# Double-width input products on GpSimd, six replica slots, output rows in the gated tile, and five state products a period on GpSimd

## The reference, cut to what matters

```python
def _mamba(x, inproj, conv_w, conv_b, xproj, dt_w, dt_b, Alog, Dp, outproj):
    u, z = jnp.split(x @ inproj, 2, axis=-1)
    uc = silu(causal_conv(u, conv_w) + conv_b)               # 512 channels
    dt, Bm, Cm = jnp.split(uc @ xproj, [16, 32], axis=-1)     # 16 states
    delta = softplus(dt @ dt_w + dt_b)
    A = -jnp.exp(Alog)
    def step(h, (u_t, d_t, B_t, C_t)):                        # along the sequence
        h = exp(d_t[..., None] * A) * h + (d_t * u_t)[..., None] * B_t[:, None, :]
        return h, einsum('bdn,bn->bd', h, C_t)
    y = (ys + uc * Dp) * silu(z)
    return y @ outproj
```

## Time and profile before

| | |
|---|---|
| median of 3 runs | 1573.46 us (1573.46 to 1575.78) |
| the profiled execution | 1577.74 us |
| its span | 1575.5 us |
| busy: PE, DVE, ACT, GpSimd | 1188.5, 1168.5, 766.0, 917.2 us |
| L1057, 256 input products on GpSimd | 597.3 us, 2364 ns each |
| L1105, 192 + 64 recurrences on DVE | 439.0 + 145.8 us |
| L1115, 192 C products on DVE | 234.9 us, 1223 ns each |
| L1063, 64 C products on GpSimd | 151.1 us, 2361 ns each |

### The profile page before, as it was taken

How to read it: one execution, slowest core, us unless ns; L and a number is a source line. 1 busy time by engine, 2 the same in 40 slices (tenths; PEclk the granted TensorE clock), 3 DMA queues, 4 the chain that set the end, 5 groups by cost and what they waited for, 6 DMA issues and landing times. The chain is left out here.

```text
span 1575.5 us, 14568 instructions
## 1 busy us (share of the span) xinstructions
PE 1188.5 (75%) x4900; PEld 663.6 (42%) x4900; DVE 1168.5 (74%) x1029; ACT 766.0 (49%) x1018; POOL 917.2 (58%) x410
## 2 busy tenths in 40 slices
PE   6899982897659887288883763445663999999998
PEld 4788820232113332033221210111232778787887
DVE  4433356999999999999999999995277654544544
ACT  5333364677555675457755554441134543333440
POOL 4420017999999999999999999983355000000000
PEclk9999995898769998698987766666885999999999
DMA  5133016442365232633233343210502230301102
GB/s 188 47 114 107 27 59 280 147 160 69 147 214 187 76 130 105 253 140 114 108 135 125 153 152 133 88 45 14 208 27 64 97 134 1 134 0 54 66 27 79
DMA packets 44415, 173.73 MB, mean 110 GB/s; under 512 B 5681, under 2 KB 10289, under 8 KB 31554
## 3 DMA queue, kind: packets, MB, share of 16 engines
q1 hardware_dynamic: 44354, 172.98, 29.8%
HBM read 138.89 MB, written 34.08 MB: 110 GB/s over the span
## 5 line engine op out<-in xcount | busy, mean ns | idle before, releaser
L1057 POOL TENSOR_TENSOR scan_dbu<-scan_rep,scan_bc 128x1024 f32<-128x1024 f32 x256 | 597.3, 2364 | 43.2 <-DMA scan_rep<-dd_rows 36.6
L996 ACT ACTIVATE scan_hs<-scan_rep,scan_neg_a 128x1024 f32<-128x1024 f32 x256 | 285.4, 1118 | 347.4 <-DVE scan_hc L1115 305.8
L1105 DVE TENSOR_TENSOR_SCAN scan_hs<-scan_hs,scan_dbu 128x1024 f32<-128x1024 f32 x192 | 439.0, 2286 | 11.3 <-ACT scan_hs L996 10.9
L904 PE MATMUL scan_ysum<-scan_hc,scan_sel 128*32 128x512 f32 x1024 | 176.3, 821 | 236.0 <-DVE scan_hc L1115 235.9
L1115 DVE TENSOR_TENSOR scan_hc<-scan_hs,scan_bc 128x1024 f32<-128x1024 f32 x192 | 234.9, 1223 | 6.1
L904 PEld LDWEIGHTS scan_ysum<-scan_hc,scan_sel 128*32 128x32 f32 x1024 | 36.3, 132 | 356.2 <-issue 356.2
L829 PE MATMUL scan_pb<-scan_xin,scan_inwf 128*128 128x512 f32 x384 | 172.8, 604 | 0.0
L1063 POOL TENSOR_TENSOR scan_hc<-scan_hc,scan_bc 128x1024 f32<-128x1024 f32 x64 | 151.1, 2361 | 12.9 <-DVE scan_hc L1105 12.6
L1105 DVE TENSOR_TENSOR_SCAN scan_hc<-scan_hs,scan_dbu 128x1024 f32<-128x1024 f32 x64 | 145.8, 2278 | 11.2 <-POOL scan_dbu L1057 11.2
L829 PEld LDWEIGHTS scan_pb<-scan_xin,scan_inwf 128*128 128x128 f32 x384 | 72.4, 193 | 103.3 <-issue 103.3
L32 PE MATMUL ffn_sl<-ffn_tanh_s,xm_s 128*128 128x512 f32 x384 | 106.0, 411 | 2.3 <-DVE ffn_tanh_s L1814 2.3
(11 more groups left out here) (186 smaller groups left out, 1626.6 us busy)
## 6 DMA issues: line engine op xcount, KB each, us to landing
scan_rep<-dd_rows SPq DMA_DIRECT2D x64, 1024.0 KB, 5.6
scan_bc<-bc_rows SPq DMA_DIRECT2D x32, 512.0 KB, 5.9
dd_rows<-scan_dd SPq DMA_DIRECT2D x16, 1024.0 KB, 3.8
ffn_wt<-in_ew SPq DMA_DIRECT2D x16, 1024.0 KB, 7.8
scan_inwf<-fold SPq DMA_DIRECT2D x12, 512.0 KB, 3.8
cond<-scan_bc SPq DMA_DIRECT2D x16, 256.0 KB, 3.2
scan_xin<-cond SPq DMA_DIRECT2D x4, 1024.0 KB, 7.5
y_all<-scan_yo SPq DMA_DIRECT2D x8, 512.0 KB, 3.1
```

Source lines behind the costliest of these rows:

```text
L904: mm = nc.tensor.matmul(ysum[i * D32:(i + 1) * D32, h, :], sel[:], hc[:, (s0 + i) % HCR, h * CT:(h + 1) * CT], start=False, stop=last, til ...
L996: nc.scalar.activation(hs[:, s % HSR, :], rep[:, e % REPS, 0, :], ACT.Exp, scale=neg_a[:, k % 2, NI * dc + i, r // NI:r // NI + 1]).then_i ...
L1057: nc.gpsimd.tensor_tensor(dbu[:, s % DBR, :], rep[:, e % REPS, 1, :], bc[:, j, 0, :], ALU.mult).then_inc(dbu_done, 1)
L1105: nc.vector.tensor_tensor_scan(states, hs[:, s % HSR, :], dbu[:, s % DBR, :], 0.0, ALU.mult, ALU.add).then_inc(scan_done, 1)
```

## The change

What it does:
- `inputs` is called for every second unit and computes two input products in one operation: 128 x 2 x 1024, the B row broadcast over both. It waits for both replicas and for both `dbu` buffers.
- `REPS` goes from 5 to 6, so that a pair lies in adjacent slots and does not wrap.
- `pool_unit`: five C products a period on GpSimd in place of four, units 0, 2, 8, 10, 13 (late periods: 0, 2, 4, 10, 13).
- `POOL_STEP_AT` (6, 7) becomes (6, 8), the late one (8, 9) becomes (8, 10), so `step_du` comes behind one more pair.
- To make room in SBUF: `yo` goes and `out_rows` writes over the last two slices of `uc`, which the output projection has read by then; so it first waits for both projections of its half. `conv` of those slices waits for the stores. `ident` lies in `hc`'s last slot. `xw` and `dtw` hold one direction and are loaded again for each group in period 2.

```diff
-REPS = 5
+REPS = 6
+POOL_UNITS, LATE_POOL_UNITS = (0, 2, 8, 10, 13), (0, 2, 4, 10, 13)
+def late_step(w):
+    return w == 0 or w % DC == DC - 1
 def pool_unit(s):
     r = s % UPP
-    return r % NI == 0
+    return r in (LATE_POOL_UNITS if late_step(s // UPP) else POOL_UNITS)
-POOL_STEP_AT, LATE_POOL_STEP_AT = (6, 7), (8, 9)
+POOL_STEP_AT, LATE_POOL_STEP_AT = (6, 8), (8, 10)
...
-        self.xw = sb("xw", [P, 2, DC, XROWS])
-        self.dtw = sb("dtw", [DTR + 1, 2, DIN])
+        self.xw = sb("xw", [P, DC, XROWS])
+        self.dtw = sb("dtw", [DTR + 1, DIN])
...
+    def load_row_weights(self, sp, a, k):
+        sp.dma_start(self.xw[:], a["xw"][:, k % 2]).then_inc(self.rows_w_in, 16)
+        sp.dma_start(self.dtw[:], a["dtw"][:, k % 2]).then_inc(self.rows_w_in, 16)
...
-        yo = sb("yo", [P, KC, CT])
+        ident = hc[:, HCR - 1, 0:P]
...
+        def out_place(k, h):
+            return uc[:, k % 2, DC - KC:DC, h * CT:(h + 1) * CT]
...
@@ SP, in period p of group k
+                    if p == DC - 2 and n < GROUPS:
+                        bank, use = USES["t", k, DC - 1, HALVES - 1]
+                        sp.wait_ge(bank_ready[bank], use)
+                        ahead.load_row_weights(sp, a, n)
...
@@ ACT, conv(k, dc, h)
+                if k >= 2 and dc == DC - KC and h == 0:
+                    act.wait_ge(yo_stored, 16 * HALVES * (k - 1))
@@ ACT
             def out_rows(k, cc, h):
-                n = HALVES * k + h
-                wait(act, yo_stored, 16 * n)
+                for other in range(KC):
+                    ready(act, "o", k, other, h)
                 x, free = ready(act, "o", k, cc, h)
-                nc.scalar.activation(yo[:, cc, :], x, ACT.Copy).then_inc(free, 1)
+                nc.scalar.activation(out_place(k, h)[:, cc, :], x, ACT.Copy).then_inc(free, 1)
@@ GpSimd, inputs(s)
                 if r < NI:
-                    pool.wait_ge(rep_in[e % REPS], 16 * (e // REPS + 1))
+                    for x in (e, e + 1):
+                        pool.wait_ge(rep_in[x % REPS], 16 * (x // REPS + 1))
                 if w % DC == 0 and r % NI == 0:
                     pool.wait_ge(bc_in[j], 2 * 16 * (w // DC + 1))
-                wait(pool, scan_done, s - DBR + 1)
-                nc.gpsimd.tensor_tensor(dbu[:, s % DBR, :], rep[:, e % REPS, 1, :], bc[:, j, 0, :], ALU.mult
-                                        ).then_inc(dbu_done, 1)
+                wait(pool, scan_done, s + 1 - DBR + 1)
+                nc.gpsimd.tensor_tensor(dbu[:, s % DBR:s % DBR + 2, :], rep[:, e % REPS:e % REPS + 2, 1, :],
+                                        bc[:, j, 0, :].unsqueeze(1).to_broadcast([P, 2, SEQ]), ALU.mult
+                                        ).then_inc(dbu_done, 2)
@@ GpSimd, the loop over units
-                    inputs(s)
+                    if r % 2 == 0:
+                        inputs(s)
@@ DVE, weigh(s)
+                if s == HCR - 1:
+                    dve.wait_ge(diag_done, 2 * DC)
```

More of the change, by code:

```diff
@@ L590, in __init__ @@
         self.stored = [[ctx.enter_context(nc.semaphore(f"scan_stored{d}_{cc}")) for cc in range(KC)] for d in range(2)]
-        self.vecs, self.inwz_in, self.folded = (ctx.enter_context(nc.semaphore("scan_" + n)) for n in ("vecs", "inwz_in", "folded"))
+        self.vecs, self.inwz_in, self.folded, self.rows_w_in = (
+            ctx.enter_context(nc.semaphore("scan_" + n)) for n in ("vecs", "inwz_in", "folded", "rows_w_in"))
         self.inwf_in = [ctx.enter_context(nc.semaphore(f"scan_inwf_in{i}")) for i in range(IWR)]
@@ L595, in load_vectors @@
     def load_vectors(self, sp, a):
-        for dst, name in ((self.vec, "vecs"), (self.neg_a, "alog"), (self.one_row, "one_row"), (self.xw, "xw"), (self.dtw, "dtw"),
-                          (self.taps, "taps")):
+        for dst, name in ((self.vec, "vecs"), (self.neg_a, "alog"), (self.one_row, "one_row"), (self.taps, "taps")):
             sp.dma_start(dst[:], a[name]).then_inc(self.vecs, 16)
+        self.load_row_weights(sp, a, 0)
+    def load_row_weights(self, sp, a, k):
+        sp.dma_start(self.xw[:], a["xw"][:, k % 2]).then_inc(self.rows_w_in, 16)
+        sp.dma_start(self.dtw[:], a["dtw"][:, k % 2]).then_inc(self.rows_w_in, 16)
     def load_z_weights(self, sp, a, k):
@@ L630, in mamba_phase @@
         outw = sb("outw", [P, DC, DM])
-        ident, sel = sb("ident", [P, P]), sb("sel", [P, D32])
+        sel = sb("sel", [P, D32])
         diag = sb("diag", [P, 2, DC, P])
@@ L646, in mamba_phase @@
         pb = ps("pb", [P, 2, CT])
-        vecs, inwz_in, inwf_in, xin_in = ahead.vecs, ahead.inwz_in, ahead.inwf_in, ahead.xin_in
+        vecs, inwz_in, inwf_in, xin_in, rows_w_in = ahead.vecs, ahead.inwz_in, ahead.inwf_in, ahead.xin_in, ahead.rows_w_in
         consts_in, outw_in, zeroed, neg_done, diag_done = (sem(n) for n in (
@@ L747, in store_out @@
                 freed(sp, *(("o", k, cc, h) for cc in range(KC)))
-                sp.dma_start(y_all[k][:, :, h * CT:(h + 1) * CT], yo[:]).then_inc(yo_stored, 16)
+                sp.dma_start(y_all[k][:, :, h * CT:(h + 1) * CT], out_place(k, h)).then_inc(yo_stored, 16)
             def z_used(k):
@@ L753, in z_used @@
                     sp.wait_ge(bank_ready[bank], use)
-            for dst, name in ((ident, "ident"), (sel, "sel")):
-                sp.dma_start(dst[:], a[name]).then_inc(consts_in, 16)
+            for dst, name in ((ident, "ident"), (sel[:], "sel")):
+                sp.dma_start(dst, a[name]).then_inc(consts_in, 16)
             store_rows(0)
@@ L847, in first_x_proj @@
                     for h in range(HALVES):
-                        mm = nc.tensor.matmul(out[h][0][0:XROWS, :], xw[:, 0, dc, :], uc[:, 0, dc, h * CT:(h + 1) * CT],
+                        mm = nc.tensor.matmul(out[h][0][0:XROWS, :], xw[:, dc, :], uc[:, 0, dc, h * CT:(h + 1) * CT],
                                               start=(dc == 0), stop=(dc == DC - 1))
@@ L855, in x_proj @@
                 out, done = claim(("x", k, h))
+                pe.wait_ge(rows_w_in, 2 * 16 * (k + 1))
                 wait_uc(pe, k, range(DC))
                 for dc in range(DC):
-                    mm = nc.tensor.matmul(out[0:XROWS, :], xw[:, k % 2, dc, :], uc[:, k % 2, dc, h * CT:(h + 1) * CT],
+                    mm = nc.tensor.matmul(out[0:XROWS, :], xw[:, dc, :], uc[:, k % 2, dc, h * CT:(h + 1) * CT],
                                           start=(dc == 0), stop=(dc == DC - 1))
@@ L864, in step_size @@
                 freed(pe, *(("x", k, i) for i in range(HALVES)))
-                nc.tensor.matmul(out, dtw[:, k % 2, dc * P:(dc + 1) * P], dbl[0:DTR + 1, h * CT:(h + 1) * CT],
+                nc.tensor.matmul(out, dtw[:, dc * P:(dc + 1) * P], dbl[0:DTR + 1, h * CT:(h + 1) * CT],
                                  start=True, stop=True).then_inc(done, 1)
@@ L910, in _ @@
             does = {"u": in_proj, "x": x_proj, "t": step_size, "z": z_gate, "o": out_proj, "skip": skip}
-            pe.wait_ge(vecs, 6 * 16)
+            pe.wait_ge(vecs, 4 * 16)
+            pe.wait_ge(rows_w_in, 2 * 16)
             pe.wait_ge(inwf_in[0], 16)
@@ L1021, in _ @@
                 k, p = divmod(w, DC)
-                step_in_at, exp_at, ln_at = LATE_STEP_AT if p + 1 == DC or w == 0 else STEP_AT
+                step_in_at, exp_at, ln_at = LATE_STEP_AT if late_step(w) else STEP_AT
                 for r in range(UPP):
@@ L1068, in _ @@
             pool.wait_ge(consts_in, 2 * 16)
-            pool.wait_ge(vecs, 6 * 16)
+            pool.wait_ge(vecs, 4 * 16)
             for d in range(2):
                 for dc in range(DC):
-                    nc.gpsimd.tensor_scalar(diag[:, d, dc, :], ident[:], vec[:, d, 1, dc:dc + 1], None, ALU.mult
+                    nc.gpsimd.tensor_scalar(diag[:, d, dc, :], ident, vec[:, d, 1, dc:dc + 1], None, ALU.mult
                                             ).then_inc(diag_done, 1)
             for w in range(PERIODS):
-                add_at, du_at = LATE_POOL_STEP_AT if w % DC == DC - 1 or w == 0 else POOL_STEP_AT
+                add_at, du_at = LATE_POOL_STEP_AT if late_step(w) else POOL_STEP_AT
                 for r in range(UPP):
                     s = UPP * w + r
-                    inputs(s)
+                    if r % 2 == 0:
+                        inputs(s)
                     if s >= POOL_LAG and pool_unit(s - POOL_LAG):
```

2 lines of the change are left out of this document (1 added, 1 removed).

## The result

The changed kernel is slower: median 1584.97 us against 1576.26 us for the kernel before, six runs each; ratio 1.0059, 95% interval 1.003 to 1.0088. The three runs of before that the forecast started from had a median of 1573.46 us, so the forecast (1577.5, a ratio of 1.0026) had the direction right and the size too small: +3.9 us forecast, +8.7 between the medians, +8.4 between the two profiled spans (1583.9 and 1575.5).

A forecast was written before the change was run, and what follows sets the result against it. DVE bounds the kernel before; GpSimd, at 52.1 us a period, becomes the bound. Head to last period +0.1, replicas +2.7, tail +1.1 make +3.9 us: 1581.6 profiled, 1577.5 against the median; range 1564 to 1588.

The forecast's parts named there:

- DVE sets the pace before, GpSimd just behind.: Periods of the kernel before: DVE needs 51.6 us, GpSimd 50.8, measured 52.26.
- The price of a pair, 4.49 us.: GpSimd's double input product: issued 4.49 us apart, likely span 4.43 to 4.60, from a fixed part of 0.13 us.
- GpSimd is the bound, 52.1 us of work a period.: Changed kernel's periods: GpSimd's eight pairs and seven single operations take 52.1 us, more than DVE's 50.3.
- The head, +4.5 us.: Start of the stretch: the first pair needs two replicas, and period 1's first scan comes 4.5 us later.
- The replicas at the boundaries, 0.9 us each.: Three group boundaries: GpSimd waits for replicas behind the later step_du, 0.9 us each, 2.7 us together.
- I count GpSimd as never waiting for DVE.: Inside periods: DVE frees a pair's buffers 0.6 to 4 us ahead; its other waits fall in 1.8 us of slack.
- Output rows and SBUF room, 0 inside.: Group periods: later copies and reloads hide in DVE's slack and cost 0, otherwise 2.6 us at most.
- the rival of the late replicas: Group boundaries: the row store, beside B and C loads, costs 3.8 us more each, 11 in all; 1589 us, chance 0.15.
- The tail, +1.1.: End of the stretch: TensorE's third product starts 0.6 us late and the last copies add 0.5 us; +1.1 us.
- The last period, -1.3.: Period 15: GpSimd has no step operations, DVE leads, and the C product taken from it gives back 1.28 us.
- the forecast case: Whole kernel: pair price of 4.45 to 4.53 us, giving 1572 to 1582 us; chance 0.44.
- the pair saves nothing: GpSimd's pairs: cost 4.62 us, periods 53.1, total 1593 us, or 1585 at 4.55; chance 0.10.

The follow-up runs named there:

- e2: Kernel before with five C products a period on GpSimd (units 0, 2, 8, 10, 13) and single input products; 1.0077 of before.
- e8: Changed kernel with the first four input products of all as single operations; 1.0042 of before.
- e3: Changed kernel with single input products, the old four C units and old step places, leaving the SBUF room and sixth slot; 0.9995 of before.
- e9: Changed kernel with ACT's output copies each one unit later in periods 4, 8 and 12; 1.0052 of before.
- e1: Changed kernel with four C products on GpSimd (0, 2, 8, 10; late 0, 2, 4, 10), unit 13's given back to DVE; 1.0068 of before.
- e5: The changed kernel again, unaltered, as a control; 1.0050 of before.
- e6: Changed kernel with unit 2's C product on DVE in periods 4, 8 and 12 alone; 1.0030 of before.
- e11: e10 with the first four input products single and step_du of late periods before the pair; 1.0035 of before.
- e12: Kernel before with six C products on GpSimd in the very last period alone; 0.9979 of before.
- e4: Changed kernel with step_du of the late periods before the pair, late places (8, 9); 1.0035 of before.
- e7: Changed kernel, pairs kept, with the four C products of before (units 0, 4, 8, 12); 1.0084 of before.
- e10: Changed kernel with five C products only in each group's two middle periods and the last of all, four elsewhere; 1.0033 of before.

## Why the prediction was right, and where it fell short

- *DVE sets the pace before, GpSimd just behind.* Right; e2 shows that GpSimd can't take another product.
- *The price of a pair, 4.49 us.* Measured 4.49, from start to start of the next operation. The first pair, the only one that ran beside an idle DVE, lasts 4.50 us; this agrees with the 4497 ns of the Trainium skill (GPSIMD Engine Reference, 3.1). All pairs together last 4.549 us, 0.06 longer than their spacing, so the 4.45 that I worked out from the figure was too low.
- *GpSimd is the bound, 52.1 us of work a period.* Right to 0.1 us, gate to gate (52.0 in plain periods) and in the sum above.
- *The head, +4.5 us.* Right, +4.5. Its cause was also right in the sum (pairs start late, then GpSimd's pace): 2.2 us go from period 1's first scan when the first four products are single (e8).
- *The replicas at the boundaries, 0.9 us each.* This is the term that was too small: 2.7 us forecast, 5.5 measured. The forecast took the landings from the start of the kernel, two replicas 11.3 us behind the end of `step_du` and four 19.0 with the B and C rows ahead. They landed after 11.4, 13.0 and 11.5 us, and after 19.5, 20.5 and 19.1, and a pair starts 0.2 us behind the landing. "That just fits for the first pair" left nothing over, and the first pair waited each time. The store took 3.8 us, so this is not the rival of the late replicas.
- *"I count GpSimd as never waiting for DVE."* Not quite right: 0.45 us ahead of period 15 in this profile. The reason given, that DVE's waits for ACT fall in its slack of 1.8 us a period, fails where the stall is 2.67 us: DVE was 0.95 us late there, and only the later replica hid it.
- *Output rows and SBUF room, 0 inside.* Right: e3, e9.
- *The tail, +1.1.* It was +2.9 in the profile. The first 16 output projections took 8.5 us, not 7: TensorE's granted clock was 0.64 of full speed in the 5 us from 1097 on, and 1.00 in those of the kernel before, though both stood at 0.50, the lower of the two levels (1.2 GHz), 3 us ahead of the last gate, behind a wait of TensorE of 8.9 us in both. The other runs separate the two shares. Where the clock is at 1.00 (2.4 GHz) by 1 us behind the last gate, the old tail takes 19.5 us (before) and the new one 21.0 (e1, e5, e6, e8, e9, e11). Where it rises some 4 us behind the gate, the old one takes 20.95 (e12) and the new one 22.4 (the changed kernel; e3, e4, e7 and e10 have 22.5 to 22.8). So 1.5 us is the change's and the rest the clock's; e2, with the old tail and 0.50 and then 0.77, took 22.6. Why the clock rose later in some executions stays open.
- *The last period, -1.3.* It was -2.1: before, DVE also lost 1.4 us to ACT in it, after 0.4.
- *Size.* Forecast +3.9; the terms that it lacked are 2.8 us at the boundaries, and what the tail's clock and the start of the first load happened to be in the two executions. The time is inside the stated range, 1564 to 1588, but outside the 1572 to 1582 of the forecast case. Of the 7.5 us between forecast and measured, 2.8 are the base, whose median came out at 1576.26 and not 1573.46. That the range held owes something to the rivals that widened it: "the pair saves nothing" had 1585 at D = 4.55, about the measured time by a wrong mechanism, and the spacing of 4.49 rules it out.

What stays open: periods at the group boundaries are 1 to 3 us longer than plain ones in the versions with pairs. The pairs alone can't be the cause, for single products show it too: 53.1 to 53.5 us in three periods of the kernel before, 54.1 in periods of e2 and e12, while e3 has 52.9 at most. Stalls of ACT and TensorE that differ between executions are part of it; what the step of two buffers adds is argued from e7 and not shown. Six `dbu` buffers would tell, and there is no room in SBUF for them. Loading the B and C rows behind replica 3, which bears on the replicas that ended all six waits, wasn't tried.

## What to carry to other kernels

Count each engine's queue for a period in spacings, not durations, before moving work: between two full engines, an operation that frees 1.28 us on one and costs 2.31 on the other is worth it only where the other has the room, as in a last period whose preparing work falls away. Fusing two operations saves their fixed part (0.13 us here) and doubles the grain of the buffers between the engines. With the same work on both engines, pairs at uneven distances came out at 1.0084 where singles had 0.9995 (e7, e3), and pairs with one single operation to each had plain periods of 51.4 to 51.7 us in place of 52.6 (e1, e7): spread the single operations evenly.

An estimate of a landing that "just fits" is a wait: give it a price. Where an instruction waits for several things, the releaser that a profile names may not be the last; put the end of each beside the moment at which the engine was free. And a slack figure for a whole period doesn't cover a stall that is longer than it.

## What the runs showed of the hardware that I had not expected

GpSimd's two-input product is nearly all per element: 1.22, 2.31 and 4.49 us of spacing for 512, 1024 and 2048 columns leave 0.13 us that fusing can save, and a second row with a broadcast operand costs nothing extra. These pairs ran beside a DVE that was busy nearly all the time, with one operand of its scans in PSUM and one in SBUF, and their spacing is what the rows of 512 and 1024 give. A pair started 0.21 or 0.22 us behind the landing of the replica that it waited for.
